# Two chosen experts instead of all eight: tokens sorted by expert through DRAM in an attention and mixture-of-experts kernel

## The reference, cut to what matters

```python
# layer 0
router_weights = softmax(xf @ rw + rb)
topw, topi = top_k(router_weights, 2); topw = softmax(topw)
combine = zeros((T, 8)).at[arange(T)[:, None], topi].add(topw)
h = gelu(einsum('td,edf->etf', xf, w1) + b1[:, None, :])      # 128 -> 512, all 8 experts
eo = einsum('etf,efd->etd', h, w2) + b2[:, None, :]           # 512 -> 128
out = einsum('etd,te->td', eo, combine)                       # x + out is normalized after it
# layer 1
sh = silu(xf @ sh_w1.T) @ sh_w2.T                             # the shared expert
gates = zeros((n, 8)).at[arange(n)[:, None], topk_idx].set(softmax(topk_vals))
sel = einsum('ned,ne->nd', silu(einsum('nd,ehd->neh', xf, w1)) @ w2, gates)
out = sh + sel
```

## Time and profile before

| What | Value |
|---|---|
| Median of three runs | 4735.49 us (4720.38 to 4739.81) |
| Profiled execution, span | 4733.2 us |
| PE busy | 4551.8 us (96%) |
| PEld busy | 2800.6 us (59%) |
| DVE busy | 3608.6 us (76%) |
| ACT busy | 2701.6 us (57%) |
| POOL busy | 698.8 us (15%) |
| Mean granted TensorE clock | 0.980 |

### The profile page before, as it was taken

One profiled execution on the slowest core, in us unless ns is written; L12 is line 12 of the kernel. 1 busy time (PEld: TensorE's weight loads), 2 busy tenths in 40 slices (PEclk: granted clock), 3 DMA queues, 4 the chain that ended last, 5 costly groups with the idle time before them and its releaser, 6 DMA issues.

```text
span 4733.2 us, 104936 instructions
## 1 busy us (share of the span) xinstructions
PE 4551.8 (96%) x40946; PEld 2800.6 (59%) x41312; DVE 3608.6 (76%) x9823; ACT 2701.6 (57%) x5505; POOL 698.8 (15%) x853
## 2 busy tenths in 40 slices
PE   6999999999999999999999999999999999999999
PEld 3566555666655566665565556655566555655566
DVE  6867777777777777777768887788877888788875
ACT  1666666667666666665565555555555555555554
POOL 2111211211121121111110111011110111101100
PEclk8999999999999999998999999999999999999999
DMA  2222222222222222223233323332233323333222
GB/s 68 39 60 57 44 55 56 63 67 56 60 46 53 55 65 67 53 58 80 55 97 81 83 61 87 96 86 68 66 99 82 86 61 83 103 81 80 62 70 74
DMA packets 168008, 327.22 MB, mean 69 GB/s; under 512 B 25656, under 2 KB 76624, under 8 KB 167520
## 3 DMA queue, kind: packets, MB, share of 16 engines
q1 hardware_dynamic: 167184, 320.48, 27.6%
q10 hardware_dynamic: 336, 0.01, 0.0%
HBM read 237.40 MB, written 4.19 MB: 51 GB/s over the span
## 4 chain that ended last, share of the span: by engine, by line
PE 79%; DVE 14%; ACT 3%; issue 2%; SPq 1%; DMA 0%; POOL 0%; DVEq 0%
PE sums L961 16%; PE b L1022 10%; PE b L1034 10%; PE b L832 9%; PE b L943 7%; PE b L933 7%; DVE chunk_max L1075 5%; PE b L856 4%; PE b L917 3%; DVE nm_s L1064 3%; DVE b L1081 3%; PE b L884 2%; PE b L996 2%; PE b L908 2%; ACT probs_c L1232 1%
## 5 line engine op out<-in xcount | busy, mean ns | idle before, releaser
L1232 ACT ACTIVATE probs_c<-b 128x512 f32<-128x512 f32 (+1 forms) x3584 | 1738.8, 571 | 1069.0 <-PE b L943 1061.2
L1081 DVE CUSTOM_DVE_ANT_0 b<-b,mcross_q 128x512 f32<-128x512 f32 (+1 forms) x2048 | 1121.8, 605 | 211.2 <-PE b L832 208.9
L1075 DVE TENSOR_REDUCE chunk_max<-b 128x1 f32<-128x512 f32 x1536 | 973.6, 683 | 144.3 <-PE b L832 139.3
L961 PE MATMUL sums<-probs_c,vc 128*32 128x256 f32 x13312 | 932.4, 395 | 0.6 <-ACT o_c L1236 0.3
L832 PE MATMUL b<-kc,qc 32*128 32x512 f32 (+1 forms) x4096 | 820.5, 412 | 18.2 <-DVE chunk_max L1075 7.1
L1034 PE MATMUL b<-w_back,hidden 128*128 128x128 f32 x4352 | 562.3, 280 | 14.7 <-DVE vc L1138 9.2
L832 PEld LDWEIGHTS b<-kc,qc 32*128 32x128 f32 x4096 | 425.3, 187 | 250.9 <-ACT probs_c L1232 94.4
L1034 PEld LDWEIGHTS b<-w_back,hidden 128*128 128x128 f32 x4352 | 526.4, 192 | 73.3 <-ACT probs_c L1232 24.4
L961 PEld LDWEIGHTS sums<-probs_c,vc 128*32 128x32 f32 x13312 | 348.0, 111 | 341.1 <-issue 168.0
L943 PE MATMUL b<-qc,kc 32*128 32x256 f32 (+1 forms) x6656 | 514.4, 336 | 16.7 <-DVE chunk_max L1077 2.2
L1022 PE MATMUL b<-xT_e,w_in 128*128 128x256 f32 x2176 | 527.9, 387 | 0.8 <-DVE chunk_max L1081 0.7
(11 more groups left out here) (159 smaller groups left out, 4498.6 us busy)
## 6 DMA issues: line engine op xcount, KB each, us to landing
w_in<-in_experts SPq DMA_DIRECT2D x272, 256.0 KB, 3.2
w_back<-in_experts SPq DMA_DIRECT2D x272, 256.0 KB, 3.3
kc<-k_hi SPq DMA_DIRECT2D x1024, 50.0 KB
ctxT<-in_ctxT SPq DMA_DIRECT2D x32, 800.5 KB, 6.2
kc<-k_lo SPq DMA_DIRECT2D x512, 50.0 KB
mask_words<-in_mcross SPq DMA_DIRECT2D x32, 800.5 KB
mask_words<-in_mcrossT SPq DMA_DIRECT2D x32, 768.0 KB
out_x<-xe SPq DMA_DIRECT2D x32, 128.0 KB, 1.9
```

The lines of the kernel that those rows point to most:

```text
L961: last = pe.matmul(acc[HP * j:HP * j + HP, :], T["vc"][x.p][0:x.kn, v0:v0 + HP], probs_of(T, x)[0:x.kn, j, half:half + S], start=x.j == 0, ...
L1075: done = dve.tensor_reduce(best[:, x.i:x.i + 1], tile, AX, ALU.max)
L1081: done = dve.tensor_tensor_reduce(part, part, mask, 1.0, -3e38, ALU.add, ALU.max, best[:, qt:qt + 1])
L1232: act.activation(probs_of(T, x)[0:x.kn, x.j, 0:n], tile[0:x.kn, 0:n], ACT.Exp, scale=SCALE).then_inc(M["a_read"], 1)
```

## The change

Layer 0, all batches, and layer 1, its first 14, no longer multiply every token by every expert. Batches are taken in groups: six of four batches and two of three (`GROUPS`). For each batch the two choices of every token get a place in a DRAM array sorted by expert (new step `RK` on PE and DVE), POOL writes each token's row to its two places (`SCT`, indirect DMAs of 128 rows), and once a group is complete, DVE makes a table of slices (`TB`): for each slice of 128 sorted rows its first row and its expert. The number of slices is fixed at the most that can be needed, 23 for four batches and 19 for three. For each slice SP reads row and expert from the table, loads the rows (`XL`) and that expert's weights and bias (`EL`). PE transposes them (`XS`) and multiplies (`EH`, 4 matmuls of 128 columns, then `EY`, 4 of 128 columns), ACT copies the result out, and SP stores it (`YS`). Later POOL gathers each token's two results (`GA`) and DVE adds them with their weights to the batch's rows (`CB`), which waited in DRAM (`KP`, `XB`). In layer 1 the shared expert is still applied to all tokens, at a fixed weight, and batches 14 and 15 keep all nine experts (`dense`).

Places of other side work in a round, the planned lengths and two of the planner's constants change as well, and the sorted arrays are filled with zeros in rounds 0 to 3. Only `xe` and the bias table lose their second buffer or their resident copy.

```diff
+GROUPS = [range(0, 4), range(4, 8), range(8, 12), range(12, 16), range(16, 20), range(20, 24), range(24, 27),
+          range(27, 30)]
+SLICES = [(len(group) * S * TOPK + E0 * (P - 1)) // P for group in GROUPS]
-LENGTH = (140.4, 145.8)
+LENGTH = (127.0, 134.6)
-NEAR, AHEAD, SOON, MOST, SLACK = 0.0436, 167.5, 0.32, 3, 2
+NEAR, AHEAD, SOON, MOST, SLACK = 0.0571, 179.0, 0.32, 3, 2
...
-WHEN = [{"experts": (0.207, 1.0), "keys": (0.177, 0.426), "values": (0.198, 0.975), "self": (0.08, 0.58), ...
-        {"experts": (0.079, 1.0), "keys": (0.293, 0.368), "values": (0.119, 0.401), "self": (0.029, 0.629), ...
+WHEN = [{"route": (0.084, 0.484), "keys": (0.177, 0.43), "values": (0.233, 1), "self": (0.014, 0.607),
+        {"route": (0.042, 0.451), "keys": (0.552, 0.562), "values": (0.119, 0.34), "self": (0.029, 0.629),
+WORKED = [[(4, 4, 0.553, 1), (5, 6, 0, 1), (6, 6, 0, 1), (7, 6, 0, 1), (8, 1, 0, 0.2)],   # round, slices, from, to
...
+          [(28, 7, 0, 1), (29, 7, 0, 1), (30, 5, 0, 0.4)],
+          [(30, 4, 0.55, 1), (31, 11, 0, 1), (32, 4, 0, 0.3)]]
+COMBINED = {0: (8, 0.443, 0.718), 1: (9, 0.419, 0.729), ...                            # batch: round, from, to
...
+        elif x.kind == "RK":                                   # PE
+            pe.matmul(tile[:, 0:E0], T["up_to"][:], picks[:, 0, :], start=True, stop=True)
+            ...                                                # five bf16 matmuls of 8 columns
+        elif x.kind == "EH":
+            for f in range(NF):
+                last = pe.matmul(tile[:, f * P:(f + 1) * P], T["w_in"][load.slot][:, f * P:(f + 1) * P],
+                                 T["xT_slice"][x.j][:], start=True, stop=True)
+        elif x.kind == "EY":
+            for f in range(NF):
+                last = pe.matmul(tile[:, 0:D], hid[:, f * P:(f + 1) * P], T["w_back"][load.slot][:, f * D:(f + 1) * D],
+                                 start=f == 0, stop=f == NF - 1)
...
+        elif x.kind == "EH" and x.l == 0:                      # ACT
+            act.wait_ge(M["bias_loaded", x.slot], 16 * x.of["load"].k0)
+            for f in range(NF):
+                done = act.activation(T["hidden"][x.slot][:, f * P:(f + 1) * P], tile[:, f * P:(f + 1) * P], ACT.Gelu,
+                                      bias=T["b_slice"][x.slot][:, f:f + 1])
...
+        if x.kind == "SCT":                                    # POOL
+            pool.wait_ge(M["pos_made"], nth(x.of["rk"]))
+            wait_made(pool, M, x.of["payload"])
+            for k in range(TOPK):
+                for qt in range(QT):
+                    pool.indirect_dma_start(
+                        sorted_rows[x.g % 2][:], bass.IndirectOffsetOnAxis(ap=T["place"][:, x.m % B, qt, k:k + 1], axis=0),
+                        payload[:, qt, :], None).then_inc(M["scattered"], 16)
+        elif x.kind == "GA":
+            ...                                                # waits for the last stores, then four gathers alike
...
+        elif x.kind == "CB":                                   # DVE, 128x128 each
+            for k in range(TOPK):
+                for qt in range(QT):
+                    done = dve.scalar_tensor_tensor(out=back[:, qt, :], in0=sums[:, k, qt, :],
+                                                    scalar=T["gates"][:, x.m % B, qt, k:k + 1], in1=back[:, qt, :],
+                                                    op0=ALU.mult, op1=ALU.add)
...
+        elif x.kind == "XL":                                   # SP
+            sp.wait_ge(M["table_made"], nth(x.of["table"]))
+            row_of[x.g, x.i] = sp.value_load(table[0:1, 0, x.i:x.i + 1], min_val=0, max_val=SORTED_ROWS - P)
+            expert_of[x.g, x.i] = sp.value_load(table[0:1, 1, x.i:x.i + 1], min_val=x.l * E0, max_val=x.l * E0 + E0 - 1)
+            sp.wait_ge(M["scattered"], 16 * PARTS * nth(x.of["sct"]))
+            sp.dma_start(T["slice"][x.slot][:], sorted_rows[x.g % 2][bass.ds(row_of[x.g, x.i], P), :]
+                         ).then_inc(M["slice_loaded", x.slot], 16)
```

More of the change, by code:

```diff
@@ L218, in read @@
         elif kind in A_RING:
-            table = ACT.Gelu if kind == "EF" and x.l == 0 else ACT.Exp
+            table = ACT.Gelu if kind == "EH" and x.l == 0 else ACT.Exp
             drain = self.cost(ACT_US, x)
             drain = drain - 0.21 if kind == "SC" and x.last else drain
-            if kind in ("EF", "SC", "SS") and table != self.table:
+            if kind in ("EH", "SC", "SS") and table != self.table:
                 drain, self.table = drain + TABLE, table
@@ L774, in nth, with weighed, needs_weights @@
     return x.n + 1
+def weighed(n):
+    return sum(needs_weights(m) for m in range(n + 1))
+def needs_weights(n):
+    return n < B or n not in GROUP_OF
 def in_ring(x):
```

624 lines of the change are left out of this document (478 added, 146 removed), and 13 rows, old and new, of tables (COMBINED, FILL, WORKED).

## The result

The changed kernel takes 5214.99 us (median of 4 runs, 5211.18 to 5228.46) beside 4734.83 us (4720.38 to 4739.81) for the kernel before: the ratio is 1.102, 95% interval 1.0997 to 1.1047. It is 10% slower, where 4300 us were forecast. Its profiled span is 5210.1 us, 476.9 us over the 4733.2 of before.

A forecast was written before the change was run, and what follows sets the result against it. PE was taken as the first bound, with DVE close in places. From 4733 us: 525 net PE saving off, plus 17 rank step, 12 and 42 given back, 15 clock, 6 end, giving 4300 us; own range 4240 to 4360, high end 4430.

The forecast's parts named there:

- Work of each engine: Forecast busy work: DVE about 3440 us, ACT near 2610, POOL 190 more for indirect DMAs, PE near 4100.
- SP: hidden, as long as no wait in the queue holds the key moves: On SP's queue, slice commands add 10 to 19 us a round, hidden, costing nothing.
- Rival D: SP's queue: slice loads waiting there delay key moves; slower from 14.4 us a round, 4900 us with 20; chance 0.03.
- The clock, 15 us: PE's clock: thinner PE work costs 1 us for each of 15 rounds, 15 us.
- rival B: PE's clock falls to 0.90 in layer 0: 96 us more, 4396 us; chance 0.08.
- the sum's term for 176: PE's added slices: 2.00 to 2.29 us each, 352 to 403 us for 176.
- PE, removed: PE's expert matmuls: 272 pairs of batch and expert at 3.51 to 4.01 us go, 955 to 1090 us.
- the 12 and 42 us: Given back to DVE's limit: 12 us in rounds 1 to 3, 42 us over 14 rounds of layer 1.
- I take nothing: POOL's queue: indirect DMAs ahead of query and key splits cost no time, bound 0 to 300 us.
- rival C: POOL's indirect DMAs delay the query and key splits: 150 us, 4450 us; chance 0.07.
- The end: Last round: serial store, gather, add and store of the last batches, 6 us more.
- Rival A: DVE becomes the bound over whole rounds, its share stuck at 80%: 4372 us; chance 0.20.

The follow-up runs named there:

- e15b: e14 with layer 0's slices due by 0.88 of a round, and layer 1's in rounds 23 and 27 by 1.0: 4445.82 us, ratio 0.938.
- e1: The changed kernel with the key moves, and all waits on them, left out: 4766 us.
- e4: The changed kernel with a 12 us pause of other work planned between a layer 0 slice's load and its transpose: 5120 us.
- e11: The changed kernel, order planned with a model of SP's queue, 12 us pause before transposes, 8 us before a layer 0 burst's last result: 4765 us.
- e9: The kernel before with 4 of 8 experts in layer 0 and 5 of 9 in layer 1, no sorting: 4424 us.
- e6: The changed kernel without POOL's scatters and gathers, neither issued nor waited for: 5030 us.
- e16b: The changed kernel with one edit, each slice's result stored at once instead of one slice later: 5007 us.
- e13: e12 with layer 0's order made as in the kernel before: 4671 us, ratio 0.986.
- e12: The changed kernel with dense experts in layer 0, sorted slices in layer 1 alone, their loads and stores planned on ACT's queue: 4832 us, ratio 1.021.
- e5: The changed kernel with the first eight matmuls of each slice done twice: 5145 us.
- e14: e11 with each slice's result stored at once instead of one slice later: 4575 us.
- e17b: The kernel of e14 again, in three rounds for an interval: 4577.84 us, ratio 0.966.

## Why the prediction was wrong

**Work of each engine: right.** DVE within 10 us, ACT within 47, POOL within 37. In e15b even the time comes near: PE's busy time, with the 15 us for the clock, was forecast at 4551.8 - 525 + 17 + 15 = 4058.8 us, and is 4099.1, 40 more; its idle time at 181.4 + 12 + 42 + 6 = 241.4, and is 343.1, 102 more. That is the whole distance from 4300 to the 4442.2 of e15b's span. The distance from there to the changed kernel, 768 us, is waits (534 us of idle time, the 78 in stalls among them) and busy time (234 us, with the same instructions: the clock).

**"SP: hidden, as long as no wait in the queue holds the key moves": the step that failed.** The 1108 us of waiting in the earlier trace rows were read as room. They are the opposite: SP waits there at the head of an in-order queue for a step of PE, and a row load behind it goes out only after that wait and the 12 moves. The commands' own time, put at 10 to 19 us a round, is not what failed: with the key moves left out the same commands leave 39.4 us of waits for rows (e1). Their place is: the planner took a row load to be ready a fixed time after PE had reached it. The wait that the sum put at nothing cost PE 248.7 us for rows, 85.4 for `w_back` and 37.8 for `slice_sum`, and the clock behind these. Rival D had the queue right and its victim wrong. It made the key moves late; what were late were the slice loads (15.0 us a round in rounds 4 to 15), the stores (292.9 us of ACT's time) and the masks (137.8 us of DVE's). It said slower from 14.4 us a round; 27 of the 30 rounds became longer, and its chance of 0.03 was far too small. The lever is the order of the same instructions: the queue's model with e4's lead gives 432 us (the missing stalls included), e11's pause 18, the store at once 187, the earlier end of the bursts 132, in sum the 769 between 5215 and 4446.

**"The clock, 15 us": mis-sized, rival B.** B had 0.90 in layer 0 for 96 us; it was 0.824, and three untouched groups cost 188.9 us more. A slice cost 2.76 us and not 2.00 to 2.29, at least 83 us over the sum's term for 176. Most of it goes with the waits: with these gone, e15b has 0.936 in layer 0, 345 us at the low level in place of 1246, 30 us more than before in the three groups, and 2.59 us a slice. Not all: e9, without any slice, has 0.950, where the kernel before has 0.967. The page "TensorE: Matmul & The Clock Gate" of the Trainium skill, section "HAM oscillation — how this bites in real kernels", describes bursts of matmuls shorter than the DMA waits between them, each of which begins at the lower clock. The trace agrees: 0.50 for the 8.8 us behind the wait of 14.37 us.

**"PE, removed": right as work, too high as time.** e9 gives 2.41 us a pair where the forecast had 3.76, or 3.4 when the 54 us given back are spread over the 140 pairs that its 525 us are worth. The forecast's own rows, DVE 89% busy without experts and 54% with them, pointed that way; the 12 and 42 us were too small. e9, without sorting, has 98 us more idle time than the kernel before, 44 over these 54. That is less than half of the 102 us above; 46 more are e15b's waits for `w_back` and rows.

**POOL: "I take nothing": too little; rival C's way did not come.** The indirect DMAs in the changed kernel (ns: least, median, most):
```profile
L1632 POOL DMA_INDIRECT expert_sums<-sorted_sums,place x120: 940/953/1402, 1261.5 to 5204.2; - x120
L1621 POOL DMA_INDIRECT sorted_rows<-xe,place x64: 953/966/1233, 250.0 to 2620.5; - x64
```
They take 0.95 us and more, not 0.79. C had PE wait for the splits, and PE's waits for anything of POOL are 7.1 us in all. What came beside the bursts are the stalls, with 78 us of PE's idle time in this trace and none in e15b's. The 185 us of e6 hold both; what the DMAs cost without the stalls stays open.

**The end.** Forecast +6 us, measured +56.6, and still +37 in e15b (193.1 against 155.8 us): the last slices, store, gather, add and store follow one another.

**Rival A** did not come: DVE is at 66%, and at 77% in e15b.

What stays open is the rest of a group's end in layer 0, 5 to 7 us, what the stalls are, and how the clock's loss divides between the waits and PE's thinner work. Whether the order alone makes the changed kernel slow on a chip without stalls is settled in the main by e16b: 5007 us, one late store less and otherwise the changed kernel, is still 271 us over the kernel before.

## What to carry to other kernels

Before a change that adds commands to an in-order queue is judged, ask of each what stands ahead of it, for what that waits, and which buffer it holds until it is done; the queue's waiting time is no room. Let whatever makes the order know the queue, rather than move the commands to an engine that computes: here one set of instructions on the same queues took 5215 or 4446 us, and the same steps in a planned order took 4770 us with the loads on ACT's queue and 4578 on SP's. Don't judge a change by its first order, nor by half of the causes removed: after e13 the sorted form seemed to lose in layer 0, and one late store and the end of a burst had made it so. And before a difference between two runs is put down to the edit, compare their waits: here one kind came and went with the occasion and was worth as much as several of the edits.

## What the runs showed of the hardware

- In the changed kernel a register load on SP took 0.27 us at the median of 352, and up to 1.67 us right behind queued DMAs.
- An indirect DMA of 128 rows cost POOL 0.95 to 0.98 us at the median, up to 1.40.
- In the changed kernel, in e1 to e4, e12 and e13, PE, DVE and ACT stood together for up to 6 us beside bursts of such DMAs; in e5 to e11 and e14 to e17b, on other chips, they did not.
- In the changed kernel the clock fell for 3.4 to 37.5 us at a time, 1246 us in all.
